# A four-layer graph network on one core: who weighs the nodes' own rows between attention layers, and where the statistics gathers stand

## The reference

```
h = (x @ W_i).reshape(n, H, C)                      # H = 4 heads of C = 32
e = leaky(es[src] + ed[dst]); m = segment_max(e, dst)
p = exp(e - m[dst]); alpha = p / segment_sum(p, dst)[dst]
out = segment_sum(alpha * h[src], dst) + b_i        # edges include node -> itself
x = elu(out)
```

## Time and profile before

| | us |
|---|---|
| median of 3 runs (8997.59 to 8999.83) | 8999.58 |
| the profiled execution | 9000.72 |
| its span, first to last instruction | 8998.9 |
| busy: PE 5629.9, DVE 5316.6, POOL 5114.9, PEld 4517.7, ACT 4500.7 | |
| row gathers L649, 4992 of them | 4828.3 |
| bias additions L590, 14 of them, mean 2.07 each | 29.0 |
| weighings L584, 14 of them, mean 1.80 each | 25.1 |
| statistics gathers L603, 49 of them | 51.6 |

### The profile page before, as it was taken

How to read it: one execution, slowest core, us unless ns; L and a number is a source line. 1 busy time by engine, 2 the same in 40 slices (tenths; PEclk the granted TensorE clock), 3 DMA queues, 4 the chain that set the end, 5 groups by cost and what they waited for, 6 DMA issues and landing times.

```text
span 8998.9 us, 130119 instructions
## 1 busy us (share of the span) xinstructions
PE 5629.9 (63%) x34288; PEld 4517.7 (50%) x34288; DVE 5316.6 (59%) x12552; ACT 4500.7 (50%) x8146; POOL 5114.9 (57%) x5192
## 2 busy tenths in 40 slices
PE   4999979974555555555456555655534555555556
PEld 3777646654454455555345454545434444444444
DVE  6888731124666666666466666666645555555555
ACT  2555400014565656565365555656535555555554
POOL 2000000035777777776577777777747777777770
PEclk9999989965555555555555555555555555555558
DMA  3333335503444444444244444444423333333331
GB/s 101 136 141 137 143 114 189 190 29 103 123 122 124 121 124 118 126 119 107 78 118 125 119 121 124 121 123 121 117 57 86 85 88 83 88 88 83 88 83 32
DMA packets 601478, 989.12 MB, mean 110 GB/s; under 512 B 331107, under 2 KB 455044, under 8 KB 561524
## 3 DMA queue, kind: packets, MB, share of 16 engines
q1 hardware_dynamic: 217540, 544.34, 17.4%
q0 software_dynamic: 163760, 357.05, 17.3%
q10 hardware_dynamic: 219648, 81.82, 3.4%
HBM read 758.42 MB, written 224.34 MB: 109 GB/s over the span
## 4 chain that ended last, share of the span: by engine, by line
PE 34%; DVE 18%; DVEq 15%; issue 14%; POOL 13%; DMA 5%; ACT 1%; POOLq 0%; SPq 0%; ACTq 0%
PE bank L978 14%; DVEq L1283 12%; POOL arena L649 12%; PE bank L1201 8%; DVE acc L1878 8%; DMA arena<-row_table,staged_idx 4%; PE bank L1003 3%; PE bank L1129 2%; DVE arena L1865 2%; DVE bank L1834 2%; PE bank L1141 2%; DVEq L1878 1%; DVE x_mem L1555 1%; DVEq L1870 1%; PE bank L1266 1%
## 5 line engine op out<-in xcount | busy, mean ns | idle before, releaser
L649 POOL DMA_INDIRECT arena<-row_table,staged_idx x4992 | 4828.3, 967 | 1623.9 <-issue 1476.2
L1201 PE MATMUL bank<-arena 128*128 128x136 f32 x9984 | 2500.9, 431 | 1188.9 <-DVE acc L1878 895.0
L1201 PEld LDWEIGHTS bank<-arena 128*128 128x128 f32 x9984 | 2207.9, 317 | 1374.2 <-issue 1368.9
L1878 DVE TENSOR_TENSOR acc<-acc,bank 128x136 f32 x4992 | 1477.5, 296 | 1061.9 <-issue 778.4
L805 ACT ACTIVATE pick_dist<-col,dst_local 128x128 bf16<-128x128 f32 x4992 | 1521.8, 387 | 284.1 <-issue 235.9
L978 PE MATMUL bank<-arena 128*128 128x385 bf16 (+1 forms) x7546 | 1343.1, 327 | 49.5 <-DVE arena L1659 32.9
L597 POOL TENSOR_TENSOR arena<-acc,node_stat 128x896 f32 x14 | 24.4, 1745 | 1731.8 <-POOLq L609 957.2
L978 PEld LDWEIGHTS bank<-arena 128*128 128x128 bf16 x7546 | 711.4, 98 | 476.7 <-DVE arena L1659 33.2
L1157 PE MATMUL bank<-ident,arena 128*32 128x128 f32 x624 | 161.5, 414 | 1250.2 <-DVE arena L1800 1250.2
L1865 DVE TENSOR_TENSOR arena<-arena,bank 128x528 f32<-128x528 f32 x1248 | 829.3, 685 | 0.3
L1797 DVE TENSOR_TENSOR arena<-arena 128x128 f32<-128x128 f32 x156 | 60.9, 390 | 1281.8 <-DMA arena<-row_table,staged_idx 1281.8
(11 more groups left out here) (355 smaller groups left out, 5856.1 us busy)
## 6 DMA issues: line engine op xcount, KB each, us to landing
arena<-dst_rows SPq DMA_DIRECT2D x156, 1024.0 KB, 5.8
cell_rows<-arena SPq DMA_DIRECT2D x76, 1568.0 KB, 5.2
arena<-cell_rows SPq DMA_DIRECT2D x76, 1568.0 KB, 6.5
arena<-row_table,staged_idx POOLq DMA_INDIRECT x4992
edge_stats<-x_mem ACTq DMA_DIRECT2D x416, 192.0 KB
x_mem<-in_edge_attr SPq DMA_DIRECT2D x208, 192.0 KB, 2.6
x_mem<-segment_flags SPq DMA_DIRECT2D x416, 96.0 KB, 3.0
arena<-change_rows SPq DMA_DIRECT2D x312, 64.0 KB
```

What stands on the lines that cost most here:

```text
L649: pool.indirect_dma_start(gathered[:, at, :], None, table, bass.IndirectOffsetOnAxis(staged_idx[:, at:at + 1], 0)).then_inc(att_gathered[n ...
L1201: mm = pe.matmul(region(k)[:, 0:ROW], pick[:, k, :], gathered[:, b * GROUP + k, :], start=True, stop=True)
L1878: done = dve.tensor_tensor(row, row, region(m * BATCH + k), ALU.add)
```

## The change

GpSimd no longer computes in the table stages: `own_rows` is gone, with its semaphore `own_ready`. VectorE's branch for the last layer becomes the only one, so in all three stages it weighs the own rows into `xc` and adds the bias, with a drain between. The extra count that GpSimd gave to `n3.summed` is dropped, and with it the `FREE` in ScalarE's wait. The 49 gathers of `node_stats` stand in a row behind GpSimd's last row gather of layer 1 and behind two waits, for the stores of `edge_stats` and for the carry; they wait for nothing of the table stage.

```diff
--- before.py
+++ after.py
@@ -350,7 +350,7 @@
         n1 = sems("n1", "degrees inverted prefixed prefix_used scaled turned copied product taken joined")
         n2 = sems("n2", "scaled turned copied product gelu joined gathered_sums colsum centred squares "
                         "summed colvar colroot norm_ready x_done")
-        n3 = sems("n3", "scored weights weighed own_ready summed joined elu next turned copied hidden relu "
+        n3 = sems("n3", "scored weights weighed summed joined elu next turned copied hidden relu "
                         "product added stats_gathered stored")
         st = sems("stats", "x_kept loaded0 loaded1 scanned turned copied stored0 stored1 carried "
                            "carry_spread bound_loaded joined x_back")
@@ -580,16 +580,6 @@
                                         bass.IndirectOffsetOnAxis(chunk_idx[:, KB + k:KB + k + 1], 0)
                                         ).then_inc(pre.rows_gathered, 16)
 
-            def own_rows(eng, n, i):
-                eng.tensor_tensor(xc[:, :, :].rearrange("p t (h c) -> p t h c", h=HEADS),
-                                  H[:, bass.ds(i * TG, TG), 0:AW].rearrange("p t (h c) -> p t h c",
-                                                                            h=HEADS)[:, :, :, 0:HC],
-                                  att_w[:, 5, bass.ds(i * TG, TG), :].unsqueeze(3).to_broadcast([P, TG, HEADS, HC]),
-                                  ALU.mult)
-                eng.drain()
-                return eng.tensor_tensor(xc[:, :, :], xc[:, :, :],
-                                         att_bias[:, n, :].unsqueeze(1).to_broadcast([P, TG, D]), ALU.add)
-
             def scale_sums(s, i):
 
                 pool.wait_ge(s.turned, 2 * i + FREE)
@@ -649,27 +639,12 @@
                                 pool.indirect_dma_start(gathered[:, at, :], None, table,
                                                         bass.IndirectOffsetOnAxis(staged_idx[:, at:at + 1], 0)
                                                         ).then_inc(att_gathered[n][b], 16)
-                if n < LAYERS - 1:
-
-                    if n == 0:
-                        pool.sem_inc(n3.summed, FREE)
-                    pool.wait_ge(n3.weighed, n + 1)
-                    if n == STATS_LAYERS - 1:
-                        for i in range(NTG):
-                            pool.wait_ge(n3.summed, n * NTG + i + FREE)
-                            pool.sem_inc(tick, 1)
-                            own_rows(pool, n, i).then_inc(n3.own_ready, 1)
-                            if i == 0:
-                                for stored in st_stored:
-                                    pool.wait_ge(stored, 32 * (SCANS // 2 + FREE))
-                                pool.wait_ge(st.carried, 1)
-                            node_stats(i)
-                    else:
-                        with pool.Fori(0, NTG) as i:
-                            pool.wait_ge(n3.summed, n * NTG + i + FREE)
-                            pool.sem_inc(tick, 1)
-                            own_rows(pool, n, i).then_inc(n3.own_ready, 1)
-
+                if n == STATS_LAYERS - 1:
+                    for stored in st_stored:
+                        pool.wait_ge(stored, 32 * (SCANS // 2 + FREE))
+                    pool.wait_ge(st.carried, 1)
+                    for i in range(NTG):
+                        node_stats(i)
 
 
         @block.scalar
@@ -880,7 +855,7 @@
                     act.sem_inc(n3.elu, FREE)
 
                 def exp_min(i):
-                    act.wait_ge(n3.summed, n * NTG + i + 1 + FREE)
+                    act.wait_ge(n3.summed, n * NTG + i + 1)
                     act.wait_ge(n3.elu, n * NTG + i + FREE)
                     act.sem_inc(act_tick, 1)
                     nc.scalar.activation(sq[:, :, :], H[:, bass.ds(i * TG, TG), 0:D], ACT.Relu, scale=-1.0)
@@ -1953,17 +1928,13 @@
                     sums = heads(acc_t[:, bass.ds(i * TG, TG), :])[:, :, :, 0:HC]
                     dve.tensor_tensor(sums, sums, att_w[:, 4, bass.ds(i * TG, TG), :].unsqueeze(3)
                                       .to_broadcast([P, TG, HEADS, HC]), ALU.mult)
-                    if n == LAYERS - 1:
-                        own = xc[:, :, :].rearrange("p t (h c) -> p t h c", h=HEADS)
-                        dve.tensor_tensor(own, heads(H[:, bass.ds(i * TG, TG), :])[:, :, :, 0:HC],
-                                          att_w[:, 5, bass.ds(i * TG, TG), :].unsqueeze(3)
-                                          .to_broadcast([P, TG, HEADS, HC]), ALU.mult)
-                        then()
-                        dve.tensor_tensor(xc[:, :, :], xc[:, :, :],
-                                          att_bias[:, n, :].unsqueeze(1).to_broadcast([P, TG, D]), ALU.add)
-                    else:
-                        dve.wait_ge(n3.own_ready, n * NTG + i + 1)
-                        dve.sem_inc(dve_tick, 1)
+                    own = xc[:, :, :].rearrange("p t (h c) -> p t h c", h=HEADS)
+                    dve.tensor_tensor(own, heads(H[:, bass.ds(i * TG, TG), :])[:, :, :, 0:HC],
+                                      att_w[:, 5, bass.ds(i * TG, TG), :].unsqueeze(3)
+                                      .to_broadcast([P, TG, HEADS, HC]), ALU.mult)
+                    then()
+                    dve.tensor_tensor(xc[:, :, :], xc[:, :, :],
+                                      att_bias[:, n, :].unsqueeze(1).to_broadcast([P, TG, D]), ALU.add)
                     then()
 
                     done = dve.tensor_tensor(H[:, bass.ds(i * TG, TG), 0:D].rearrange("p t (h c) -> p t h c", h=HEADS),
```

## The result

The changed kernel takes 8954.81 us (median of 6 runs, 8953.19 to 8964.23), the kernel before in the same runs 8999.44. The medians lie 44.63 us apart, 0.50%; the ratio of all the runs is 0.9954, with a 95% interval of 0.9942 to 0.9965, clear of no change. The forecast was 8959 and the range 8950 to 8973.

The account below looks back on a forecast made before the run. The kernel is shared among all engines; GpSimd was taken to set the second stage, VectorE, stretched by GpSimd, the first. Gains of 3.3 and 37.4 us, sum 40.7, took the median 8999.58 to 8959 us, range 8950 to 8973.

Parts of the forecast that it names:

- The second stage: After attention layer 1, first weighing to next row gather: 118.50 us falls to 81.1, a gain of 37.4.
- VectorE's last-layer form: Stage behind the last attention layer: VectorE alone takes 3.33 us from weighing to sum, expected in both changed stages.
- the tail to the last copy: End of each stage, from group 4's product to ScalarE's copy of the last one: 20.60 us.
- The first stage: After attention layer 0, first weighing to next row gather: 84.40 us falls to 81.1, a gain of 3.3.
- TensorE's own pace: TensorE's loop with ScalarE's two copies: 26.5 us for three steps, taken as slower than VectorE's 24.3.
- The contention: First stage's VectorE round of 8.89 us: 2.95 us is stretching by GpSimd's tensor instructions, removed by the change.
- The gathers: Moved ahead of the second stage: 49 take 63.6 us, end 20.7 us before needed, cost nothing.
- The upper bound: Second stage: five long VectorE instructions a round each hold one gather 0.74 us, adding 20.7 us to the gathers.
- The rival of starved gathers: Second stage: VectorE holds up the gathers past the need, time 8959 to 8997; chance 0.08.
- The rival that gathers hold VectorE: Second stage: each gather holds VectorE its whole 1.30 us, stage 144.7 us, time 9022; chance 0.03.
- Slow TensorE: Both stages: every TensorE step takes 9.81 us, stage 88.0 us, time 8973; chance 0.14.
- The total: Gains of both stages together, 3.3 and 37.4 us: 40.7 us off the whole kernel.

Follow-up runs that it names:

- e4b: Changed kernel with all 49 gathers waiting for the last group's sum, on a chip of the usual speed: 8988.43 us.
- e3b: Changed kernel with gathers in rounds of seven, the first after the weights, each further seven after the previous group's sum: 8964.37 us.
- e5: Changed kernel plus two GpSimd tensor instructions a group on data of its own in the first stage, nobody waiting for them: 8970.06 us.
- e7: Changed kernel without the bias addition of layers 0 and 1: 8947.42 us.
- e8: Changed kernel with TensorE and ScalarE loops written out and two alternating buffers for the turned group: 8956.07 us; kernel before on that chip 9010.41.
- e8b: The kernel of e8 again, beside the changed kernel on another chip: 8944.09 us against 8957.61.
- e2: Kernel before with only the 49 gathers moved ahead, own rows left on GpSimd: 10367.32 us on a chip where the kernel before takes 10336.72.
- e1: Kernel before with own rows taken off GpSimd after layer 0 only: 10336.26 us on a chip where the kernel before takes 10336.72.

## Why the prediction was right

**The second stage**: predicted 81.1 us, measured 81.19, and 81.23 in the repeat. The sums of groups 0 to 3 (L1940) start 3.39, 11.09, 18.77 and 26.82 us after the first weighing, against the computed 3.33, 11.03, 18.73 and 26.83. That VectorE's last-layer form could be read off made the term exact. Behind it the agreement to 0.1 us is partly luck: TensorE's three steps took 27.07 us instead of 26.5, the tail to the last copy 20.25 instead of 20.60 and the rest 5.34 instead of 5.43.

**The first stage**: predicted 81.1, measured 79.57; in other runs with the same first stage 80.25, 80.41 and 81.92 (the changed kernel again, e4b, e3b). The term that was a little off is TensorE's own pace, 26.5 us for three steps; it took 24.81 in the changed kernel's profile, and VectorE's 24.3 was the other bound. Taking the slower of the two paces made the forecast 1.5 us too long. In the repeat and in e3b the three steps took 25.89 and 27.42 us, so 26.5 lies within the spread of the runs, and 79.57 is the shortest of them.

**The contention**: 2.95 us a round predicted as removed. The round is 7.99 instead of the predicted 8.10, and e5 puts 3.1 us back by GpSimd's instructions alone. The rule of the Trainium skill (SBUF — State Buffer, "Who interferes with whom"), that a VectorE instruction with two SBUF inputs and a GpSimd instruction that reads SBUF exclude one another, is borne out by e5's 1.67 and 1.80 us, where 0.19 is the time alone.

**The gathers**: they start as predicted (3.4 us after the carry against 3.2), end 69.1 us after the first weighing against the predicted 60.5, and are hidden. The term was mis-sized inside its bounds: 14 of 49 gathers take 1.28 to 1.86 us, 7 did before; the whole takes 71.9 us instead of 63.6. The gathers' busy time grew by 57.3 - 51.6 = 5.7 us and the gaps by 2.6. Of these, 1.8 us are a misreading of the earlier trace rows: the "DVE arena L1969 1.8" taken off as a wait for VectorE is six gaps of 0.30 us, as long as every other gap between two gathers, and stayed. The upper bound had 28 more held gathers and 20.7 us. The rival of starved gathers is thus true in kind and short of mattering by 12 us. A round holds two gathers, not the five of the upper bound; the last section says why. The 3100 ns of the Trainium skill's "A bandwidth-pool intuition that's wrong" (SBUF — State Buffer) were not reached: the slowest of the 49 takes 1.86 us.

**The rival that gathers hold VectorE** did not come: VectorE's long instructions are 1.08 to 1.16 us beside them. **Slow TensorE** came in part: two of three steps in the second stage are 9.80 and 9.68 us, near the rival's 9.81, with the product at a granted clock of 0.50. The forecast's 26.67 of the earlier trace rows held one such step. That not every step is slow kept the stage at 81 instead of 88, and e7, e8 and e8b show that TensorE's loop was the bound beside VectorE's.

**The total**: 42 us from the two stages against the predicted 40.7. The remaining 3 us between 8954.8 and the forecast's 8959 are smaller than the spread of the six runs (8953.19 to 8964.23) and are put down to no cause.

## What to carry to other kernels

When two engines share a step, look at what else stands in the helper's queue: seven gathers between two short instructions made a step that VectorE does in 2.2 us cost 8. Work taken off the critical path must be moved so that what others wait for comes first: the gathers alone moved ahead lost 26 us of the second stage, the own rows alone moved away gained all that was gained there. And an idle GpSimd may be worth more than a helping one, when its tensor instructions exclude VectorE's.

## What the runs showed of the hardware that was not expected

A gather issued by GpSimd beside VectorE's long instructions on two SBUF inputs takes up to 1.86 us instead of 0.94, but only 14 of 49 are held though VectorE is busy on such instructions for more than half of each round. The changed kernel's rows show when. Each of the 14 ends 0.81 to 0.84 us after the end of a long VectorE instruction that was running when it began, and so do the seven in the kernel before. A gather that begins less than 0.13 us before that end loses nothing. A held gather and its gap last 1.58 to 2.17 us, as long as two long instructions or a little less, so the five long ones that follow one another in a round (some 5 us) hold two gathers and not five, in each of the six such rows of five; one more is held before them and one after them. Three gathers that began 0.02 to 0.04 us after a long instruction were not held, and that instruction took 1.14 to 1.16 us instead of 1.08 or 1.09. Which part of the gather meets VectorE was not tried. The Trainium skill (SBUF — State Buffer, "Who interferes with whom") infers that such instructions leave descriptor generation alone; its rule on GpSimd instructions that read SBUF would fit, since a gather reads its row numbers (`last_row`) from there. 1.86 against 0.94 says only that the gather as a whole is not left alone.

The same kernel took 8999 us on one chip and 10337 on another, while stages of its form were about as long on both: 84.40 and 85.20 us for the first (e2), 118.41 and 118.44 for the second (e1). On the slow chip a ScalarE instruction whose input had been ready for 50.3 us ran 8 us after the last gather; such waits are found there all over the run and on the other chips nowhere.
